# A router that handles two row groups at once in every second step

## What is computed

```
x = x + deform_conv3x3(ln_c(x))                       # layer 0, convolution
t = tokens(x)                                         # one token = one pixel, 128 channels
p = softmax(ln_t(t) @ router_w + router_b)            # 8 experts
top 2 of p, divided by their sum
t = t + sum over the two of p_k * (ln_t(t) @ expert_w[k] + expert_b[k])
x = x + real(ifft2(mix(fft2(ln_c(x)))))               # layer 1: alphas and betas over channels
t = tokens(x)
logits = ln_t(t) @ gate_w.T + gate_b                  # 64 experts, softmax over the 16384 tokens
per image and expert: the 8 best tokens, pooled, a two-matmul MLP with gelu, scattered back
x = x + that
```

## Time and profile before

| | |
|---|---|
| median of 3 runs | 3808.22 us (3803.49 to 3808.84) |
| profiled execution, whole time | 3802.93 us |
| its span, first to last instruction | 3801.1 us |
| busy in the span: PE, DVE, ACT, POOL | 3507.7, 2906.9, 1781.2, 1812.1 us |
| mean granted TensorE clock | 0.953 |

### The profile page before, as it was taken

How to read it: one execution, slowest core, us unless ns; L and a number is a source line. 1 busy time by engine, 2 the same in 40 slices (tenths; PEclk the granted TensorE clock), 3 DMA queues, 4 the chain that set the end, 5 groups by cost and what they waited for, 6 DMA issues and landing times. The chain is left out here.

```text
span 3801.1 us, 90975 instructions
## 1 busy us (share of the span) xinstructions
PE 3507.7 (92%) x30743; PEld 2369.3 (62%) x30743; DVE 2906.9 (76%) x9434; ACT 1781.2 (47%) x5461; POOL 1812.1 (48%) x3052
## 2 busy tenths in 40 slices
PE   5999999999999999999968999999999999996668
PEld 4767777776777677777635555555555555554445
DVE  5677677777676777777648999999999999995634
ACT  3444444444444444444303555555555555555234
POOL 4666656666566665666523444333444333444210
PEclk8999999999999999999979999999999999997855
DMA  5555554555545545555437777777777777784789
GB/s 121 131 125 131 127 122 123 122 139 121 125 122 131 129 118 126 128 124 121 91 132 274 269 274 273 276 278 275 274 271 276 272 278 278 287 307 139 269 323 395
DMA packets 666788, 750.50 MB, mean 197 GB/s; under 512 B 105697, under 2 KB 532961, under 8 KB 649938
## 3 DMA queue, kind: packets, MB, share of 16 engines
q1 hardware_dynamic: 560850, 670.71, 56.5%
q10 hardware_dynamic: 104448, 71.85, 6.2%
q0 software_dynamic: 1024, 2.10, 0.2%
HBM read 552.46 MB, written 181.50 MB: 193 GB/s over the span
## 5 line engine op out<-in xcount | busy, mean ns | idle before, releaser
L421 PE MATMUL a_sb<-a_sr,wcv 128*128 128x512 f32 (+3 forms) x2820 | 1052.0, 515 | 0.8 <-DVE a_xo L557 0.8
L403 PEld LDWEIGHTS a_sb<-a_tt,a_win 32*128 32x128 f32 x19008 | 642.8, 186 | 122.0 <-issue 121.9
L421 PEld LDWEIGHTS a_sb<-a_sr,wcv 128*128 128x128 f32 x2820 | 492.9, 190 | 335.0 <-issue 289.9
L403 PE MATMUL a_sb<-a_tt,a_win 32*128 32x144 f32 (+1 forms) x19008 | 661.8, 292 | 23.6 <-ACT a_yr L462 8.2
L1226 DVE TENSOR_TENSOR b_P<-b_P,b_x 128x1024 f32<-128x1024 f32 x512 | 620.2, 1212 | 1.6 <-DMA b_P<-pd 1.3
L480 ACT COPY a_sr<-a_sb 128x432 f32<-128x432 f32 (+14 forms) x1172 | 363.5, 389 | 394.6 <-PE a_sb L403 394.6
L509 DVE COPY a_sr<-a_sb 128x432 f32<-128x432 f32 (+14 forms) x1172 | 419.3, 413 | 138.4 <-PE a_sb L403 128.6
L435 ACT ACTIVATE a_tn<-a_sb,a_rs 128x128 f32<-128x128 f32 x512 | 192.4, 456 | 583.9 <-POOL a_rs L574 583.9
L1116 PE MATMUL b_z<-b_P,b_ew 128*128 128x512 f32 x1024 | 464.4, 596 | 0.0
L1119 PE MATMUL b_z<-b_P,b_ew 128*128 128x512 f32 x1024 | 460.3, 592 | 0.0
L1372 POOL MEMSET b_x<- 1x512 f32 x128 | 65.9, 515 | 815.2 <-DVE b_P L1226 815.2
(11 more groups left out here) (190 smaller groups left out, 5459.3 us busy)
## 6 DMA issues: line engine op xcount, KB each, us to landing
b_P<-pd SPq DMA_DIRECT2D x128, 2048.0 KB, 7.2
a_win<-xtp SPq DMA_DIRECT2D x2144, 36.0 KB
a_xin<-in_x SPq DMA_DIRECT2D x128, 256.0 KB, 3.2
xtp<-a_tn ACTq DMA_DIRECT2D x128, 256.0 KB, 4.7
x1d<-a_xo SPq DMA_DIRECT2D x128, 256.0 KB, 4.0
b_x<-x1d SPq DMA_DIRECT2D x128, 256.0 KB
x2d<-b_xa SPq DMA_DIRECT2D x128, 256.0 KB, 3.3
pw<-x3d SPq DMA_DIRECT2D x128, 256.0 KB, 6.6
```

Source lines behind the costliest of these rows:

```text
L403: t = e.matmul(d[:, 0:3 * m_, t0:3, NU_ * i:NU_ * i + nx], win[32 * q:32 * q + 32, half_of(Q, j) % NWH, NWIN // 3 * h + i, :], m, start=(j ...
L421: t = e.matmul(ob[:, r:r + m, :], k["wcv"][:, 3 * (2 - kr) + kx, :], rows[:, :, t_, :], start=(t_ == 0 and r == 0), stop=(t_ == 8))
```

## The change

In `phase_bc`, the router's small operations work on a pair of groups (2q, 2q + 1): 8 rows of 8 logits where there were 4, in the steps where G is odd. In the steps with even G the stage `weights` has only its four products. The same holds for the exponential, the turn of `pp` on PE (both groups' 64 columns side by side), the copy to `pT` and the transfer to `pd` (128 rows in place of 64). The `spread` stays one per group. For that, the products handle Z = G - 3, and `spread`, `experts`, `experts2`, `mixed`, `place`, `turn2`, `store2`, `stats2`, `turn_scale` and `LAG` have one step more of lag. `clear` goes behind `scales` in `STEP` (and its lag from 4 to 5). The gate's weights are 128x64 in place of two zero-padded 128x128 tiles, and its two products write to partitions 0 to 63 and 64 to 127 of one bank instead of accumulating over the whole bank. Ring sizes: NX1 10, NPT 2, NLR 10. The unused tile `mk` goes.

```diff
-LAG = 11
+LAG = 12
-NX1, NPB, NPT, NLR = 9, 3, 4, 8
-STEP = (("load", -3), ("load2", LAG - 2), ("read", 0), ("clear", 4), ("turn2", 6), ("fourier", LAG), ("turn3", LAG + 3),
-        ("store2", 6), ("turn_p", 2), ("experts", 4), ("p_out", 2), ("scales", 1), ("best", LAG + 4),
-        ("x3_sum", LAG + 1), ("mixed", 5), ("stats1", 0), ("stats2", 6), ("stats3", LAG + 1), ("x3", LAG), ("store3", LAG + 1), ("spread", 2),
-        ("norm3", LAG + 2), ("gate", LAG + 3), ("experts2", 4), ("place", 5), ("sums", LAG + 4), ("weights", 1),
-        ("turn_scale", 7), ("collect", LAG + 5))
+NX1, NPB, NPT, NLR = 10, 3, 2, 10
+STEP = (("load", -3), ("load2", LAG - 2), ("read", 0), ("turn2", 7), ("fourier", LAG), ("turn3", LAG + 3),
+        ("store2", 7), ("turn_p", 2), ("experts", 5), ("p_out", 2), ("scales", 1), ("clear", 5), ("best", LAG + 4),
+        ("x3_sum", LAG + 1), ("mixed", 6), ("stats1", 0), ("stats2", 7), ("stats3", LAG + 1), ("x3", LAG),
+        ("store3", LAG + 1), ("spread", 3), ("norm3", LAG + 2), ("gate", LAG + 3), ("experts2", 5), ("place", 6),
+        ("sums", LAG + 4), ("weights", 1), ("turn_scale", 8), ("collect", LAG + 5))
...
+            if stage in ("turn_p", "p_out") and (s - lag) % 2 == 0:
+                continue
...
             elif stage == "gate":
                 w.wait_ge(tnT3_ready, G + 1)
-                e.matmul(X[:, 0:256], gw[:, 0, :], tnT3[:, u, 0:256], start=True, stop=False)
-                e.matmul(X[:, 0:256], gw[:, 1, :], tnT3[:, u, 256:512], start=False, stop=True).then_inc(gated, 1)
+                for j in range(2):
+                    t = e.matmul(X[64 * j:64 * j + 64, 0:256], gw[:, :], tnT3[:, u, 256 * j:256 * j + 256],
+                                 start=True, stop=True)
+                t.then_inc(gated, 1)
...
-                Z, n = G - 2, R_STEPS * G + 1
-                if G < NG:
+                Z, q = G - 3, G // 2
+                v, n = q % 2, R_STEPS * q + 1
+                pair = G < NG and G % 2 == 1
+                if pair:
                     w.wait_ge(scaled, G + 1)
                     w.wait_ge(lr_ready, G + 1)
-                    e.tensor_tensor(lg[:, u], lr[:, G % NLR, :, 0:8], rs[:, u, 4:8, None].to_broadcast([128, 4, 8]), ALU.mult
-                                    ).then_inc(r_step, 1)
+                    i = (G - 1) % NLR
+                    e.tensor_tensor(lg[:, v].rearrange("p (g r) x -> p g r x", g=2), lr[:, i:i + 2, :, 0:8],
+                                    rs[:, :, 4:8, None].to_broadcast([128, 2, 4, 8]), ALU.mult).then_inc(r_step, 1)
...
-                    for r in range(4):
-                        m = e.max(mx[:, u, r, :], lg[:, u, r, :])
+                    for r in range(8):
+                        m = e.max(mx[:, v, r, :], lg[:, v, r, :])
...
-                    for r in range(4):
-                        m = e.match_replace(l2[:, u, r, :], m2[:, u, r, :], lg[:, u, r, :], -3.0e38)
+                    for r in range(8):
+                        m = e.match_replace(l2[:, v, r, :], m2[:, v, r, :], lg[:, v, r, :], -3.0e38)
...
             elif stage == "p_out":
                 w.wait_ge(x_free, users["turn_p", G] + 1)
-                w.wait_ge(P_in[(G - NPT) % NPB], 16 * ((G - NPT) // NPB + 1))
-                e.dma_start(pd[G % NPT * 64:G % NPT * 64 + 64, :], pT[0:64, G % NPT, :]
-                            ).then_inc(p_out[G % NPT], 16)
+                q = G // 2
+                for g in (G - 5, G - 4):
+                    w.wait_ge(P_in[g % NPB], 16 * (g // NPB + 1))
+                e.dma_start(pd[q % NPT * 128:q % NPT * 128 + 128, :], pT[:, q % NPT, :]
+                            ).then_inc(p_out[q % NPT], 16)
             elif stage == "spread":
-                w.wait_ge(p_out[G % NPT], 16 * (G // NPT + 1))
+                q = G // 2
+                d = q % NPT * 128 + 64 * u
+                w.wait_ge(p_out[q % NPT], 16 * (q // NPT + 1))
                 w.wait_ge(mixed, G + 1 - NPB)
```

More of the change, by code:

```diff
@@ L977, in order_b @@
         for stage, lag in STEP:
-            n = NS if stage == "scales" else NG + 2 if stage == "weights" else NG
+            n = NS if stage == "scales" else NG + 3 if stage == "weights" else NG
+            if stage in ("turn_p", "p_out") and (s - lag) % 2 == 0:
+                continue
             if 0 <= s - lag < n and not (stage == "load" and s - lag < 3):
@@ L1085, in tensor @@
         e.matmul(X[:, 8:136], k["ones"][:, :], al[:, :], start=True, stop=True)
-        e.matmul(X[:, 136:392], k["ones"][:, :], gw[:, :, :], start=True, stop=True).then_inc(summed_w, 1)
+        e.matmul(X[:, 136:200], k["ones"][:, :], gw[:, :], start=True, stop=True).then_inc(summed_w, 1)
         w.wait_ge(centred, 5)
@@ L1103, in tensor @@
             elif stage == "turn_p":
-                w.wait_ge(p_ready, G + 1)
+                w.wait_ge(p_ready, G // 2 + 1)
                 w.wait_ge(std_ready, G + 1)
-                e.transpose(X[:, 0:128], pp[:, u, :], ident[:, :]).then_inc(p_turned, 1)
+                e.transpose(X[:, 0:128], pp[:, G // 2 % 2, :, :].rearrange("p g x -> p (g x)"), ident[:, :]
+                            ).then_inc(p_turned, 1)
             elif stage == "turn_scale":
-                w.wait_ge(scaled, G + 7)
-                e.matmul(X[:, 0:4], rev[:, :], rs[:, u, 0:4], start=True, stop=True).then_inc(scale_turned, 1)
+                w.wait_ge(scaled, G + 8)
+                e.matmul(X[:, 0:4], rev[:, :], rs[:, (G + 7) % 2, 0:4], start=True, stop=True).then_inc(scale_turned, 1)
             elif stage == "experts":
                 w.wait_ge(x2_ready, G - 1)
-                w.wait_ge(x_free, users["turn_p", G] + 1)
                 w.wait_ge(z_ready, G + 1)
@@ L1153, in scalar @@
                 w.wait_ge(stats1, G + 1)
-                w.wait_ge(r_step, R_STEPS * (G - 2) + 2)
+                w.wait_ge(r_step, R_STEPS * ((G - NLR) // 2) + 2)
                 e.copy(lr[:, G % NLR].rearrange("p (a b) x -> p a b x", a=2), RD[:, :, :, 128:137]
                        ).then_inc(lr_ready, 1)
[L1157 to L1160, removed]
+            elif stage == "weights" and G < NG and G % 2:
+                q = G // 2
+                w.wait_ge(lm_ready, q + 1)
+                w.wait_ge(p_ready, q - 1)
+                e.activation(ex[:, q % 2], lm[:, q % 2], ACT.Exp).then_inc(exp_ready, 1)
             elif stage == "turn_p":
[L1162 to L1165, removed]
+                q = G // 2
+                w.wait_ge(p_turned, q + 1)
+                w.wait_ge(p_out[q % NPT], 16 * (q // NPT))
+                e.copy(pT[:, q % NPT, :], X[:, 0:128]).then_inc(x_free, 1)
             elif stage == "turn_scale":
@@ L1309, in vector @@
                 w.wait_ge(xa_ready, G + 1)
-                w.wait_ge(scaled, G + 5)
+                w.wait_ge(scaled, G + 6)
                 for r in range(4):
-                    t = e.bn_stats(st[:, u, r, :], xa[:, G % 3, r, :])
+                    t = e.bn_stats(st[:, (G + 7) % 2, r, :], xa[:, G % 3, r, :])
                 t.then_inc(stats2, 1)
@@ L1378, in sync @@
         for stage, G in order:
+            u = G % 2
             if stage == "load":
@@ L1907 @@
     arr["al"] = np.ascontiguousarray(a["L1_conv_alphas"].T)
-    arr["gw"] = np.zeros((128, 2, 128), np.float32)
-    for i in range(2):
-        arr["gw"][:, i, 64 * i:64 * i + 64] = a["L1_ffn_gate_w"].T
+    arr["gw"] = np.ascontiguousarray(a["L1_ffn_gate_w"].T)
     arr["gb"] = np.tile(a["L1_ffn_gate_b"], 2).reshape(128, 1)
```

82 lines of the change are left out of this document (44 added, 38 removed).

## The result

The changed kernel takes 3720.84 us (median, 3717.43 to 3721.86) against 3807.76 us for the kernel before on the same chip: a ratio of 0.9775, with a 95% interval from 0.9762 to 0.9789. By the medians that is 86.9 us less. The profiled execution has a span of 3719.3 us, 81.8 less than before's 3801.1. The forecast was 3695 with a range from 3668 to 3745: the time lies in the range, but outside the band of 3675 to 3715 that had a chance of 0.70, and a quarter of the forecast gain is missing. The same file in a later batch gave 3716.72 us, ratio 0.978 (0.9764 to 0.9796).

What follows compares the result with a forecast made beforehand. POOL's loop (11.65 us a step) was taken as the bound, DVE (11.29) right behind. 115 steps of 10.76 us against 1352.3 gave -114.9, ends +2: -113 us, from 3808.2 to 3695; range 3668 to 3745.

Steps and rivals of the forecast that it cites:

- What bounds the kernel: Steps of `phase_bc`: POOL's loop with `clear` in front 11.65 us, DVE 11.29, PE 10.80 to 10.96.
- Part 1: `clear` behind `scales`: takes 0.51 us out of POOL's loop; alone 0.36 us per step, then DVE is next.
- Part 2: Router in pairs on DVE: saves 1.18 us per two steps, 0.12 waiting stays; 21.52 us a pair, 10.76 a step.
- no shared cost: Rival: eight router rows cost twice four, so the pair saves nothing; 3763 us, chance 0.04.
- POOL after 4.81 - 0.51 + 0.30 = 4.60: From `best` after a step without router: POOL ready after 4.60 us, DVE after 4.48; 0.12 us wait a pair.
- Part 3: PE's `turn_p` every second step and narrower gate: own step 10.6 us, at most 10.9; gate alone worth nothing.
- PE takes over: Rival: a gate mode change costs 0.3 us, so PE needs 11.06 us a step; 3730 us, chance 0.06.
- Part 4: Weights transfer: first spread of a pair has 0.7 us cover, second over 3; no cost, bound 1.3 us a pair.
- late weights: Rival: the first spread lands too late, DVE waits once a pair; 3712 to 3770 us, chance 0.11.
- slower: Rival: spreads close together make the first land late, 10.5 us after issue; 3855 us, chance 0.06.
- Part 5: Ends around the 115 full steps: steps ahead -4 us, tail's one more step +6 us.

Runs made afterwards that it cites:

- part1_p: Kernel before with `clear` moved behind `scales`, and POOL's chain waiting for `p_ready` of the group before the last one only: 3767.6 us, ratio 0.9909.
- part1: Kernel before with `clear` moved behind `scales` and nothing else: 3807.37 us, ratio 1.0012.
- clear_front: Changed kernel with `clear` back in its old place ahead of `scales`: 3717.74 us, ratio 0.9777.
- std_pair: Changed kernel with POOL's small operation L1381 taken out of the short step, both groups' values made in the long step: 3703.95 us, ratio 0.975.
- prod_first: Changed kernel with L1381 only in the long step, for both groups, and there product 0 ahead of L1265: 3700.02 us, ratio 0.9726.

## Why the prediction was right and where it wasn't

**What bounds the kernel.** Right as an order, POOL's loop, then DVE, then PE: with POOL's wait gone (`part1_p`) a step fell to 11.38 us, of which 0.10 is idle, and 11.29 was forecast for DVE's own work. Incomplete as a description of the loop: the earlier trace rows show the memset at its head, and the prediction took it for the only thing there.

**Part 1.** "Alone this gives 0.36 us per step, then DVE is next" is wrong: `part1` gives nothing. The failed step is that the chain's other wait, `p_ready`, was listed among the stages and never given a time. It is met at 2614.85 by the rows above, the memset at 2614.87. The price of a removed wait is the distance to the next condition of the same instruction, and here that was 0.02 us. In the paired kernel the step was wrong again, for another reason (below), and there too it gave nothing (`clear_front`).

**Part 2.** The router's sizes are right to some hundredths. From the L1265 after the short step to the next L1340 it is 7.84 us in the full steps (median) (forecast: 4.56 + 3.32 = 7.88); eight MAX8 take 0.65 us (forecast: 0.66); four products without a router are 4.53 us by their starts, 2610.10 to 2614.63 (forecast: 4.56); the other stages of DVE are 4.42 to 4.48 (forecast: 4.48). DVE's own work is 21.28 us a pair, where 2 x 11.29 - 1.18 = 21.40 was forecast: -0.12. The price of four-dimensional operands, open between one and double an instruction's time, is at the low end (128x64 in 0.22 to 0.23 us), so the rival of no shared cost is out.

The failed step is "POOL after 4.81 - 0.51 + 0.30 = 4.60", counted from the start of `best`. DVE was ready after 4.48 us, exactly as forecast (2619.72 - 2614.63 - 0.61), but POOL only after 5.09. Its chain starts 0.57 us behind L1340 (2614.63 to 2615.20) where 0.12 was forecast, +0.45, and the rest of the 0.49 lies in hand-overs. `std_pair` splits it. L1381 in the short step is 0.24 to 0.25 of it: it was given no time there. The other 0.25 are small terms: the release after product 3 (0.17 us where the sum implied about 0.05), the operation of the chain beside DVE's L1329, which is 0.59 us long where the one in the kernel before, and so in the forecast, has 0.53 (free, it is 0.20), and 0.03 us of hand-over to L1265. By the rule of the shared ports, cited above, L1381 would have been held at least for the rest of one product; the prediction didn't weigh it, though the kernel before has the same situation in a milder form between the rows. DVE and POOL there:

```profile
2615.32 0.20 POOL L1353 TENSOR_SCALAR b_ss<-b_ss 128x4 f32<-128x4 f32 x1
2615.39 0.67 DVE L1317 TENSOR_TENSOR c_x<-c_x 128x512 f32<-128x512 f32 x1
2615.58 0.53 POOL L1355 TENSOR_SCALAR b_ss<-b_ss 128x8 f32<-128x8 f32 x1
2615.98 0.68 DVE L1307 TENSOR_TENSOR b_xn<-b_z,b_x 128x512 f32<-128x512 f32 x1
2616.19 0.21 POOL L1357 TENSOR_SCALAR b_ss<-b_ss 128x12 f32<-128x12 f32 x1
```

L1355 starts 0.19 us behind L1317, which adds two SBUF tiles, and is 0.53 us long, over 0.05 us after it; L1353, a like operation just ahead, takes 0.20. L1357 starts beside L1307, an addition of the same size that has one input in SBUF and the other in PSUM (`b_z`), and it isn't held: 0.21 us. This holds all through the full steps: beside L1317 no such operation took less than 0.53 us (106 of them), beside L1307 none more than 0.21 (107). Those rows were the warning.

**Part 3.** Right in size and in worth. Gate and mode changes together: from L1118 to L1113 it is 7.65 us (2606.00 to 2613.65), and in before 3.44 + 0.86 + 3.43 = 7.73, so 0.08 us a step is saved (forecast: 0.1, to less). The gate takes 0.58 (2609.53 to 2610.11), not 0.43, and the changes of mode 0.09 in front and 0.11 behind. The Trainium skill ("TensorEngine Tiling (Array Packing)", Key Properties) says a mode change drains TensorE and gives no figure; here 0.09 and 0.11 us stand at the two changes, and that they are the drain is not shown apart. With the old gate (`gate_wide`) the stretch is 7.73 us again. PE's own work is 10.7 us a step (21.89 - 0.50, by two; forecast: 10.6, at most 10.9). DVE never waits for PE in the window, so the 1.6 us by which PE falls behind were covered, and the rival "PE takes over" is out.

**Part 4.** The cover held, and by the number used. The spread of the short step is issued 5.85 us after `best` starts (2611.53; forecast: 5.89), and its weights are used 8.3 us later. The median of 8.8 us above mixes the two spreads of a pair. Taken apart, the first lands 7.3 us after its issue in the median (6.9 to 9.8; forecast: 7.2) and the second 9.9 us (8.7 to 11.5). In the step shown, the first lands at 2618.93 and the second, issued at 2617.77, at 2627.52. So the landing that grew, by 2.6 us, is that of the second, issued 6.5 us after the first (median); the forecast left it at 7.2 and gave it over 3 us of room, and that room is what took it up. DVE waited twice, 1.7 us in 41 pairs: the rivals "late weights" and "slower" did not come. `prod_first` shows how thin the cover was: half a microsecond less of it cost 12 us more of waiting. SP's waits for `pd` fell from 156.7 to 79.0 us in 2200 to 3200 us, about half, as the forecast said.

**Part 5 and the sum.** The ends are right (-4.1 and +6.2 for -4 and +6), but that they agree to 0.2 us is luck: over the traces of the eight kernels with pairs the steps ahead take 111.7 to 115.7 us and the tail 70.8 to 77.8. For the full steps the error is, per pair, +0.49 for POOL, -0.12 for DVE's own work and +0.09 for the rest: 0.04 of it are the waits for weights, and 0.05 is scatter of single pairs that no row names. 57.5 x 0.46 = 26.4 us. With 0.61 in place of 0.12 the prediction's own sum would have given 3695 + 28 = 3723. That the time still lies in the range owes something to the 0.12 us a pair, 7 us in all, by which DVE's own work came out shorter than forecast.

## What to carry to other kernels

Before a wait is priced at its whole length, list every other condition of the waiting instruction with the time at which it is met; the gain is the distance to the next one, and where two are met together only an edit that removes both is worth anything. When small operations are taken from between large two-input operations of DVE, look at what POOL has to do in that stretch: here a tiny POOL operation that reads SBUF, started in a run of them, lasted until the run ended and delayed all that stood behind it in its queue. If a product is moved forward on the engine that bounds, move its transfer forward as well.

## What the runs showed of the hardware

- A run of back-to-back DVE products with two SBUF inputs held a POOL operation with SBUF inputs until the run ended: 4.20 us for a 128x4 operation that takes 0.21 otherwise. One DVE memset of 0.07 us inside the run let it in (0.78 us).
- One DVE addition with two SBUF inputs (L1317, 0.67 us) held a small POOL operation as well: 0.53 us or more in 106 of 106. The same addition with one input in PSUM (L1307) did not: 0.21 us at most in 107.
- POOL's memset, which reads nothing, was never held: 0.51 to 0.52 us in all 128 cases, many of them beside a product.
- POOL's power held no product. In `prod_first` 113 products start before a power has ended, by 0.06 us in the first rows there and by up to 1.57 us in the second, and each still takes 1.20 to 1.23 us, with the power at 2.27 at most. Why the power, which reads SBUF as well, holds none of them, no run here tells.
- Of two broadcasts of 2 MB issued 6.5 us apart, the first landed after 7.3 us in the median and the second after 9.9, where single ones 11.65 us apart took 7.2. What makes the second slower was not tested; in the step shown it is issued before the first has landed.
